# A fused attention and mixture layer: a new order of the work of one step on all five engines

## The reference

```python
def reference(x, ...):
    h = conv1d(x, weight, groups=4, taps=9) + ctx          # (128, 32, 512)
    q = h @ dequant(q_codes, q_scales)                     # 32 heads of 128
    k = h @ dequant(k_codes, k_scales)                     # 8 heads of 128
    v = h @ dequant(v_codes, v_scales)                     # 8 heads of 128
    q, k = rope(q), rope(k)                                # xe*cos - xo*sin, xo*cos + xe*sin
    scores = q @ k.T * 128 ** -0.5 + causal_mask           # 4 q heads share one k and v head
    out = softmax(scores) @ v
    x = x + out.reshape(...) @ dequant(o_codes, o_scales)
    y = mixed_1x1_conv(x, cond)                            # weights from a small softmax
    return x + y @ base_W.T + lora(y, top2_gates)
# dequant: (codes - 8) * scale, a scale for each 128 rows of the input
```

## Time and profile before

| | us |
|---|---|
| median of 3 runs | 1638.66 |
| lowest, highest | 1638.43, 1641.78 |
| span of the profiled execution | 1638.1 |
| PE busy in it | 1605.0 |
| DVE, ACT, POOL busy in it | 1399.9, 1252.8, 1132.7 |

### The profile page before, as it was taken

The page is one execution under the profiler, slowest core; times in us unless marked ns, Lnnn a source line. Parts: engine busy times, 40 slices in busy tenths (PEclk is TensorE's granted clock), DMA queues, the critical chain, the costliest instruction groups (busy, mean ns, idle before and its releaser), DMA issues.

```text
span 1638.1 us, 37768 instructions
## 1 busy us (share of the span) xinstructions
PE 1605.0 (98%) x14878; PEld 892.8 (54%) x14878; DVE 1399.9 (85%) x2176; ACT 1252.8 (76%) x2158; POOL 1132.7 (69%) x942
## 2 busy tenths in 40 slices
PE   9989999999999999999999999999999999899999
PEld 8845555555555555555555555555555555566665
DVE  5868888888888888888888888888888888878887
ACT  3458888888888888888888888888888888532222
POOL 1077778877787778777877787778777787633332
PEclk9999999999999999999999999999999999999999
DMA  8401000001000100010001000100000002022221
GB/s 306 138 4 38 11 24 2 27 14 34 1 28 14 34 1 28 14 34 2 27 15 33 2 27 14 34 2 27 14 1 28 25 7 86 27 71 85 78 78 52
DMA packets 32317, 60.83 MB, mean 37 GB/s; under 512 B 11512, under 2 KB 14392, under 8 KB 31888
## 3 DMA queue, kind: packets, MB, share of 16 engines
q1 hardware_dynamic: 32144, 58.42, 10.9%
HBM read 47.46 MB, written 10.95 MB: 36 GB/s over the span
## 4 chain that ended last, share of the span: by engine, by line
PE 66%; DVE 16%; POOL 6%; issue 5%; ACT 1%; DVEq 0%; POOLq 0%
PE banks L840 17%; PE banks L755 16%; PE banks L780 10%; DVE q_sin L1129 9%; PE banks L769 5%; PE banks L896 5%; DVE accT L1192 4%; PE banks L799 4%; PE banks L825 3%; DVE pT L1178 2%; PE banks L939 2%; PE banks L881 2%; POOL q_f L1400 2%; PE banks L867 1%; POOL k_f L1385 1%
## 5 line engine op out<-in xcount | busy, mean ns | idle before, releaser
L755 PE MATMUL banks<-hT,w_q 128*128 128x512 f16 x2048 | 547.1, 380 | 8.5 <-DVE q_sin L1129 4.8
L1523 ACT ACTIVATE banks<-banks,ratios 128x512 f32<-128x512 f32 x768 | 503.4, 664 | 61.8 <-PE banks L755 53.1
L840 PE MATMUL banks<-o_hl,w_o 128*128 128x512 f16 x2048 | 545.2, 380 | 3.2 <-ACT banks L1533 1.5
L1533 ACT ACTIVATE banks<-banks,ratios 128x512 f32<-128x512 f32 x768 | 481.8, 660 | 43.5 <-PE banks L840 40.7
L1400 POOL TENSOR_TENSOR q_f<-q_f,q_sin 128x1024 f32<-128x1024 f32 x128 | 301.5, 2356 | 78.4 <-DVE q_sin L1129 78.4
L840 PEld LDWEIGHTS banks<-o_hl,w_o 128*128 128x128 f16 x2048 | 180.8, 98 | 262.5 <-issue 35.4
L1129 DVE TENSOR_TENSOR q_sin<-banks,rope_q 64x1024 f32<-64x1024 f32 x256 | 312.7, 1222 | 8.2 <-POOL q_f L1400 2.6
L755 PEld LDWEIGHTS banks<-hT,w_q 128*128 128x128 f16 x2048 | 189.1, 98 | 237.1 <-ACT banks L1523 34.2
L780 PE MATMUL banks<-w_v,hT 128*128 128x128 f16 x3072 | 194.2, 220 | 0.0
L1120 DVE TENSOR_SCALAR banks<-banks,ratios 128x512 f32<-128x512 f32 x192 | 145.2, 756 | 54.4 <-PE banks L769 54.4
L780 PEld LDWEIGHTS banks<-w_v,hT 128*128 128x128 f16 x3072 | 178.3, 98 | 22.0 <-issue 0.5
...
## 6 DMA issues: line engine op xcount, KB each, us to landing
...
```

The lines of the kernel that those rows point to most:

```text
L755: mm = pe.matmul(banks[:, tile], w.q[:, n[2], kt * RF * HD + tile * HD:kt * RF * HD + (tile + 1) * HD], hT[:, n[1], kt, hp], start=kt == 0 ...
L840: mm = pe.matmul(o_bank(tile), w.o[:, p[2], h * D + tile * P:h * D + (tile + 1) * P], o_hl[:, op, h], start=h == 0 and op == 0, stop=op == ...
L1523: act.activation(banks[:, tile], banks[:, tile], ACT.Copy, scale=w.ratios[:, n[0], tile, kt:kt + 1]).then_inc(q_scaled[tile], 1)
L1533: act.activation(o_bank(tile), o_bank(tile), ACT.Copy, scale=w.ratios[:, p[0], RF + tile, h:h + 1]).then_inc(o_scaled[tile], 1)
```

## The change

No computation is added or taken away. `body` gets a fourth step, r = n - 3, since the last pair of output tile 2 and the additions of output tiles 2 and 3 move into the next body. On PE the first half of v's projection goes ahead of the values, and pairs of projection and output trade places. On DVE the two additions stand between the cosine and the sine of pair 1, and the mask ahead of `scale_k(n, 0)`. On POOL `add_q` of pair 1 goes ahead of k's cosine and `normalize` ahead of `v_low`; making v's weights is split over three steps instead of one. ACT scales in the order in which PE now writes. Waits that others imply are left out. Behind the loop the pair and the additions left over from the third-last step (BEFORE) stand in the same places.

```diff
-    def make_v(self, pool, g):
+    def make_f(self, pool, g):
+        pool.tensor_scalar(self.f[:], self.codes[:, 0, KT * HD:], -8.0, WSCALE, ALU.add, ALU.mult).then_inc(self.piece_done, 1)
+
+    def make_v_high(self, pool, g):
         pool.wait_ge(self.v_s_loaded, 16 * (g + 1))
-        pool.tensor_scalar(self.f[:], self.codes[:, 0, KT * HD:], -8.0, WSCALE, ALU.add, ALU.mult).then_inc(self.step, 1)
-        pool.wait_ge(self.step, 3 * g + 1)
+        pool.wait_ge(self.piece_done, PIECES * g + 1)
         pool.tensor_tensor(self.f[:], self.f[:], self.v_s[:], ALU.mult).then_inc(self.step, 1)
-        pool.wait_ge(self.step, 3 * g + 2)
+        pool.wait_ge(self.step, 2 * g + 1)
         pool.tensor_copy(self.v[:, g % 2, 0], self.f[:]).then_inc(self.step, 1)
-        pool.wait_ge(self.step, 3 * g + 3)
-        pool.tensor_tensor(self.v[:, g % 2, 1], self.f[:], self.v[:, g % 2, 0], ALU.subtract).then_inc(self.piece_done, 1)
+
+    def make_v_low(self, pool, g):
+        pool.wait_ge(self.step, 2 * g + 2)
+        return pool.tensor_tensor(self.v[:, g % 2, 1], self.f[:], self.v[:, g % 2, 0], ALU.subtract)
 
...
-                if at(n):
-
+                if at(n) and tile in (0, 3):
+
+                    pe.wait_ge(q_sin_done[tile // 2], at(n))
                     pe.wait_ge(q_cos_done[tile // 2], at(n))
...
-                pe.wait_ge(sc_read, at(i))
...
         def values(p, blocks):
 
             if blocks[0] == 0:
+                if at(p):
+
+                    pe.wait_ge(acc_added[3], at(p))
+                    pe.wait_ge(acc_added[2], at(p))
                 pe.wait_ge(p_ready, at(p) + 1)
                 pe.wait_ge(v_ready, at(p) + 1)
-                pe.wait_ge(sc_read, at(p) + 1)
                 if p != LAST:
 
-                    pe.wait_ge(q_cos_done[0], at(p) + 2)
                     pe.wait_ge(q_sin_done[0], at(p) + 2)
-                if at(p):
-
-                    for tile in (2, 3):
-                        pe.wait_ge(acc_added[tile], at(p))
...
-                for b in range(TB):
-                    pe.wait_ge(out_ready[b], at(p) + 1)
+                if tile == (1 if p not in (PRIOR, LAST) else 0):
+                    for b in (0, 2, 1, 3):
+                        pe.wait_ge(out_ready[b], at(p) + 1)
...
-        def body(n, i, p):
+        def body(n, i, p, r):
             if n:
                 project_q(n, 0, 0)
+            if r:
+                output(r, 2, 3)
+            if i:
+                project_v(i, 0)
+            if n:
+                project_q(n, 0, 1)
             if p:
                 values(p, range(TB))
             if i:
-                project_v(i, 0)
-            if n:
-                project_q(n, 0, 1)
-            if i:
                 project_v(i, 1)
             if n:
+                project_q(n, 0, 2)
                 project_q(n, 3, 0)
-                project_q(n, 0, 2)
+                project_q(n, 1, 0)
                 project_k(n, 0)
-                project_q(n, 1, 0)
                 project_q(n, 2, 0)
-            if p:
+                project_q(n, 3, 1)
+            if p:
+                output(p, 1, 0)
                 output(p, 0, 0)
-                output(p, 1, 0)
             if n:
                 project_q(n, 1, 1)
                 project_k(n, 1)
             if p:
+                output(p, 1, 1)
                 output(p, 0, 1)
-                output(p, 1, 1)
             if i:
                 scores(i)
             if p:
+                output(p, 1, 2)
                 output(p, 0, 2)
-                output(p, 1, 2)
             if n:
                 project_k(n, 2)
                 project_q(n, 1, 2)
             if p:
+                output(p, 1, 3)
                 output(p, 0, 3)
-                output(p, 1, 3)
-            if n:
-                project_q(n, 3, 1)
+            if n:
+                project_q(n, 2, 1)
                 project_q(n, 1, 3)
             if p:
+                output(p, 3, 0)
+            if n:
+                project_q(n, 0, 3)
+            if p:
                 output(p, 2, 0)
-                output(p, 3, 0)
-            if n:
-                project_q(n, 0, 3)
-                project_q(n, 2, 1)
+            if n:
+                project_q(n, 2, 2)
+            if p:
+                output(p, 3, 1)
+            if n:
+                project_k(n, 3)
             if p:
                 output(p, 2, 1)
-                output(p, 3, 1)
             if n:
                 project_q(n, 3, 2)
-                project_q(n, 2, 2)
+            if p:
+                output(p, 3, 2)
+            if n:
+                project_q(n, 2, 3)
             if p:
                 output(p, 2, 2)
             if n:
-                project_k(n, 3)
-            if p:
-                output(p, 3, 2)
-            if n:
-                project_q(n, 2, 3)
-            if p:
-                output(p, 2, 3)
+                project_q(n, 3, 3)
+            if p:
                 output(p, 3, 3)
-            if n:
-                project_q(n, 3, 3)
...
         def turn(n, pair, which, src, dst):
 
             n_parts = src.stop - src.start
-            for tile in (2 * pair, 2 * pair + 1):
-                dve.wait_ge(q_psum[tile], KT * at(n) + KT)
...
 
         def turn_cos(n, pair):
+            for tile in (0, 1) if pair == 0 else (3, 2):
+                dve.wait_ge(q_psum[tile], KT * at(n) + KT)
...
 
         def turn_sin(n, pair):
-            if n[1] == 0 and n[0]:
-                dve.wait_ge(w_ready, n[0])
-
...
-        def body(n, i, p):
+        def body(n, i, p, r):
             if i:
                 turn_cos(i, 1)
+            if r:
+                add_out(r, 2)
+                add_out(r, 3)
+            if i:
                 turn_sin(i, 1)
             if p:
                 out_low(p, 3)
+                out_low(p, 1)
                 out_low(p, 2)
-                out_low(p, 1)
                 out_low(p, 0)
-            if n:
-                scale_k(n, 0)
             if i:
                 write_mask(i)
             if n:
+                scale_k(n, 0)
                 scale_k(n, 1)
             if i:
                 scores_T(i)
@@ -1279,8 +1288,8 @@
             if n:
                 scale_k(n, 2)
             if p:
+                add_out(p, 1)
                 add_out(p, 0)
-                add_out(p, 1)
             if i:
                 softmax_sum(i)
                 softmax_inverse(i)
@@ -1290,9 +1299,6 @@
                 softmax_T(i)
             if n:
                 turn_sin(n, 0)
-            if p:
-                add_out(p, 2)
-                add_out(p, 3)
...
         def add_q(n, pair):
-            pool.wait_ge(q_cos_done[pair], at(n) + 1)
             pool.wait_ge(q_sin_done[pair], at(n) + 1)
+            if pair:
+                pool.wait_ge(k_sin_done, at(n) + 1)
             q = q_f[:, 2 * pair:2 * pair + 2]
             pool.tensor_tensor(q, q, q_sin[:], ALU.add).then_inc(q_ready[pair], 1)
...
                 if ch == 0:
                     w.make_k(pool, g + 1)
+                    w.make_f(pool, g + 1)
                 else:
-                    w.make_v(pool, g + 1)
+                    w.make_v_high(pool, g + 1)
             elif ch < 6:
+                if ch == 2:
+                    w.make_v_low(pool, g + 1)
...
-        def body(n, i, p):
+        def body(n, i, p, r):
             if i:
+                rotate_k_sin(i)
+                add_q(i, 1)
                 rotate_k_cos(i)
-                add_q(i, 1)
                 add_k(i)
-            if i:
                 dequantize(i)
-            if i:
                 shift(i)
                 v_high(i)
+                normalize(i)
                 v_low(i)
-                normalize(i)
                 p_high(i)
                 p_low(i)
             if n:
                 add_q(n, 0)
-                rotate_k_sin(n)
 
 
         add_q(FIRST, 0)
-        rotate_k_sin(FIRST)
         program(body)
 
...
-        def body(n, i, p):
+        def body(n, i, p, r):
             if n:
                 scale_q(n, 0, 0)
-            if p:
+                scale_q(n, 0, 1)
+            if p:
+                out_high(p, 3)
+                out_high(p, 0)
                 out_high(p, 1)
                 out_high(p, 2)
-                out_high(p, 3)
-                out_high(p, 0)
-            if n:
-                scale_q(n, 0, 1)
             if i:
                 move_v(i)
...
                 exp(i)
             if n:
+                scale_q(n, 2, 1)
                 scale_q(n, 3, 1)
             if p:
+                scale_o(p, 3, 0)
                 scale_o(p, 2, 0)
-                scale_o(p, 3, 0)
-            if n:
-                scale_q(n, 2, 1)
-            if p:
+            if n:
+                scale_q(n, 2, 2)
+            if p:
+                scale_o(p, 3, 1)
                 scale_o(p, 2, 1)
-                scale_o(p, 3, 1)
-            if n:
```

(10 more changed lines are left out.)

49 lines of the change are left out of this document (26 added, 23 removed).

## The result

| | before | after |
|---|---|---|
| median of the runs, us | 1638.6 | 1617.5 |
| lowest, highest | 1638.4, 1641.8 | 1616.6, 1617.9 |
| span of the profiled execution | 1638.1 | 1615.7 |
| an ordinary step | 20.72 | 20.41 |
| mean of the 61 steps | 20.80 | 20.43 |

The ratio is 0.987, with an interval of 0.985 to 0.988: 1.3% faster. In the traces the 61 steps from the second first-matmul of the values to the sixty-third fill 130.47 to 1399.41 before and 132.12 to 1378.27 after: 22.8 us less. Ahead of them stand 1.6 us more, since the values come later in a step now, and behind them 1.2 fewer: 22.4 in all. The medians differ by 21.1 only. In every run on record with both numbers the time stands 1.8 above the span, so the profiled execution of before took some 1639.9 us, over a microsecond more than its median.

A forecast was written before the change was run, and what follows sets the result against it. A 20.72 us wait loop over values, projection, sine and additions bound each step; new DVE and POOL loops gave 20.42. 61 steps plus 1.6 extras saved 21.7, start and tail 0.5; adding 0.6 to the span: 1616.5 us, 8-in-10 range 1607 to 1629.

The forecast's parts named there:

- The 0.6 that I put between span and median: Whole kernel: median of the runs, 1638.66, stands 0.6 above the profiled span; added to 1615.9 for the forecast.
- The DVE loop: DVE: cosines, sines, additions and out_low, closed through PE's output(1,0) to output(1,3), would take 20.37 us a step.
- The new borders: DVE, sine to cosine and addition to sine: each held until earlier work finishes, 0.03 us instead of -0.09.
- three tight places on PE: PE at q(0,0), tile 2's output pair and values: nominal arrival within 0.05 us of the release, nowhere over.
- The prediction's step on ACT: ACT's waits are hidden if it runs as before; last scalings land within 0.05 us of PE's need.
- POOL's loop: POOL, add_q through k's sine and cosine to add_k and PE's release: 20.30 to 20.43 us a step.
- Two of my signs: New profile: PE's idle time ahead of output(1,0), released by out_low, and ahead of the scores, released by add_k.
- Fewer waits at nothing: Removed waits on the engines, satisfied long before, cost nothing: -0.05 to 0 us a step.
- PE's floor of 20.14: PE: a step's 36 pairs of matmuls without waits take 20.14 us, the least any order could reach.
- the first rival: PE becomes the bound at 20.14 us a step: 38.8 less, 1599 us; 0.12 for 1598 to 1611.
- Weights: POOL: v's weights split over three steps, no part above about 2.2 us, shift on time; 3.4 us saved.
- The prediction followed one: Wait loop before the change: values, tile 0's last projection, pair 0's cosine and sine, additions, values: 20.72 us, the whole step.

The follow-up runs named there:

- the last experiment: Changed kernel with k's first pair behind q(2,0), v's move ahead of the last out_high on ACT, k's cosine ahead of pair 1's add_q on POOL: 1612.6 us.
- The experiments with one part alone: Kernel before with v's half ahead of values and out_high block 3 first: 1637.8 us; kernel before with only q(0,3) earlier on PE: 1639.8 us.

## Why the prediction was right, and where it was not

**The time.** 1616.5 was forecast, 1617.5 came; a step of 20.42, and 20.41 came; a span of 1615.9, and 1615.7 came. The 0.6 that I put between span and median was no property of the kernel: the profile of before was of a slower execution than the median. That makes up the 1.0 us between forecast and result.

**The DVE loop, 20.37: right**, and seen bare in the last experiment: out_low ends at 827.71, output(1,0) starts 0.06 later (0.08 forecast), then 6.08 to the addition (5.43 + 0.63), 6.68 to the cosine of pair 1 (6.66 + 0.03), and 7.54 for the rest (7.57 less that 0.03).

**The new borders, +0.03 each: right.** In DVE's rows of the changed kernel the sine of pair 0 ends at 844.19 and the cosine of pair 1 starts 0.02 later, at 844.21; the second addition ends at 826.34 and the sine starts 0.03 later, at 826.37. With -0.09 the loop would have been 20.13. This is the rule on starting quadrants that the prediction cited from the Trainium skill ("VectorE: DVE Perf Modes", "Two Vector instructions with no wait between them"); the trace agrees with it at both new borders.

**The step's bound: right number, wrong owner.** I put 20.42 down to POOL and DVE, with three tight places on PE. None of these closes at 20.41. What does is the chain over the values, four out_high, the move of v and k's first pair. The prediction's step on ACT, "hidden, if it runs as before", looked at the packed row behind exp and not at ACT's work behind the values, which now come 1.8 later in the step. The rows of before would not have given it either. In them the first out_high starts 0.89 after the values (816.98):

```profile
817.87 2.07 ACT L1538 ACTIVATE o_hl<-banks 128x512 f16<-128x512 f32 x4 [0.38 <-PE banks L825]
```

With that, an estimate from rows of before is 0.08 + 2.65 to the values + 0.89 + 1.93 for four out_high + 0.67 to k's pair + 6.72 + 0.63 + 6.66 = 20.23, below DVE's 20.37. The other 0.18 came with the new order: 0.09 ahead of the values, 0.08 more to the first out_high (0.97, now block 3's; the runs that begin with block 1 have 0.90), and 0.01 in the other links. So the mechanism of the gain was right, but that the step came out within 0.01 is in part luck: I had put 0.05 on top of DVE's 20.37 for places that do not set it. POOL's loop, put at 20.30 to 20.43, is 20.35. Two of my signs did not come for the same reason: PE idles ahead of tile 1's and k's first pairs, not ahead of output(1,0), and ahead of the scores it loses only the 0.09 that it lost before.

**Fewer waits at nothing: wrong.** With the old ones back a step is 0.08 longer, 4.6 us. What costs is which of several waits an instruction itself carries: 0.05 from the sine to q(0,0) against 0.15, where the number of waits is the same. The order rows in the section on the change show it: q_sin_done0 stood first in the list and now stands last. My bounds of -0.05 to 0 were too narrow. It did not spoil the sum, since the prediction had let q(0,0) go 0.08 behind the sine in another place, though the values of before stood 0.14 behind the addition that released them.

**PE's floor of 20.14, and the first rival: too low.** Ahead of the values and ahead of the scores 0.09 are lost in every step, where nothing is waited for: a q pair ahead of the values takes 0.53 (826.04 to 826.57), not 0.43, and 0.52 in the version with v's half and block 3 first (818.84 to 819.36), where the additions had ended 1.66 earlier. The 1.97 for two output pairs and the scores had one of these in it; the values' stood in a wait before and could not be told from it. The floor is 20.23, so the changed kernel's PE still waits 0.18 a step, and the first rival's 1599 would have been some 1605.

**Weights: right in size.** The 61 steps took 4.9 us more than 61 ordinary ones before and 1.0 after: 3.9 went where I took 3.4. Of these 2.9 lie in the six steps that made v's weights (21.20 each, now ordinary); the other 1.0 went with the new order, since it stays away when the weights are made in one step again. The parts fit, and shift idles in each of the 61 steps. Undone in the new order it costs 7 us, more than the 2.9 that these steps cost before, since there is no slack left to take a late shift up.

**What was missed is how many chains before had.** The prediction followed one, over values, q(0,3), sine and additions. There were four side by side: from the values or from output(0,0), over q(0,3) or over output(2,3), through the additions. The two over q(0,3) were 20.72; the two over output(2,3) stood at 20.61 and rose to 20.80 when q(0,3) alone was moved. It named none of the other three, nor that the change brings q(0,3) nearer to the scores, on which its DVE loop rests: that pair is there just 0.06 ahead of need. The experiments with one part alone, each of which left two of the four closed, gave -1 us and +1 us, neither clear of nothing. v's half opens the two that start at the values; the earlier q(0,3) shortens the two that run over it; the additions behind the cosine take the fourth. Undone one at a time in the changed kernel they cost 85, some 16 and 8 us, so the additions matter least: 13 of the 21 us are there without them. No experiment makes just these three moves, so how much the remaining swaps of pairs and scalings bring stays open, and so does the part of the mask and of `normalize`, which were never moved back alone; some of the last pairs of a step took 0.49 to 0.58 instead of 0.43 before (0.24 in all) and don't after, so they may be needed too.
